# A four-layer perceiver on one core: layer 3's keys and values made ahead in layer 2's self-attention, and scores on 64 feature rows in layers 2 and 3

## The reference

```
# layer 2: x = x + xattn(layernorm(x), ctx, bias)
q, k, v = heads(x_q @ Wq.T), heads(ctx @ Wk.T), heads(ctx @ Wv.T)
p = softmax(q k^T / sqrt(8) + bias[b, h]);  o = p v
...  # then its own norm, a 512-wide gelu part and a second norm
# layer 2 self-attention: softmax(q k^T) + relative position bias, over the 64 tokens of a pair
# layer 3: x = x + xattn(layernorm(x), ctx), with bq, bk, bv, bo and no bias over positions
```

## Time and profile before

| | us |
|---|---|
| median of 3 runs | 1271.48 (1268.71 to 1274.01) |
| profiled execution, first to last instruction (span) | 1270.3 |
| PE busy in it | 1149.3 (90%) |
| DVE, ACT, POOL busy | 697.9, 613.0, 380.3 |

### The profile page before, as it was taken

One profiled execution on the slowest core, in us unless ns is written; L12 is line 12 of the kernel. 1 busy time (PEld: TensorE's weight loads), 2 busy tenths in 40 slices (PEclk: granted clock), 3 DMA queues, 4 the chain that ended last, 5 costly groups with the idle time before them and its releaser, 6 DMA issues.

```text
span 1270.3 us, 27700 instructions
## 1 busy us (share of the span) xinstructions
PE 1149.3 (90%) x9353; PEld 829.9 (65%) x9353; DVE 697.9 (55%) x2032; ACT 613.0 (48%) x1296; POOL 380.3 (30%) x551
## 2 busy tenths in 40 slices
PE   7879999999998879999988268899999999999888
PEld 4446666878785546788865054577777667888655
DVE  5674455554554543777775163533333346777673
ACT  4542224434333433777764132534343446777663
POOL 2300002111121274455540160304040505555350
PEclk9979999999999789999999669999999999999999
DMA  8600121222220003355520301011211110111100
GB/s 251 235 1 25 38 67 32 54 52 52 62 68 1 2 1 108 103 149 145 146 68 1 50 3 42 26 50 50 61 45 56 50 55 22 31 33 29 30 3 17
DMA packets 64837, 73.53 MB, mean 58 GB/s; under 512 B 6144, under 2 KB 57392, under 8 KB 64376
## 3 DMA queue, kind: packets, MB, share of 16 engines
q1 hardware_dynamic: 61480, 64.03, 18.6%
q0 software_dynamic: 1376, 7.49, 1.8%
q10 hardware_dynamic: 1904, 0.98, 0.5%
HBM read 69.86 MB, written 0.52 MB: 55 GB/s over the span
## 4 chain that ended last, share of the span: by engine, by line
PE 77%; DVE 7%; ACT 6%; issue 4%; POOL 3%; DMA 3%; ACTq 1%; POOLq 0%; SPq 0%; DVEq 0%
PE PS L504 14%; PE PS L516 13%; PE PS L1096 8%; PE PS L791 4%; PE PS L755 4%; PE PS L1106 4%; PE PS L507 2%; PE PS L798 2%; PE PS L742 2%; PE PS L1079 2%; ACT AR L1263 2%; PE PS L1126 2%; PE PS L1086 2%; ACT XN L1263 2%; DMA AR<-AR 1%
## 5 line engine op out<-in xcount | busy, mean ns | idle before, releaser
L516 PEld LDWEIGHTS PS<-WB,AR 128*128 128x128 f32 x1568 | 189.9, 192 | 43.6 <-issue 39.5
L516 PE MATMUL PS<-WB,AR 128*128 128x128 f32 x1568 | 190.1, 275 | 0.0
L1263 ACT ACTIVATE AR<-PS,WB 128x512 f32<-128x512 f32 x160 | 110.0, 688 | 153.2 <-PE PS L504 146.7
L1096 PE MATMUL PS<-AR 128*128 128x257 f32 x512 | 138.5, 393 | 2.6 <-POOL AR L2645 2.5
L1855 DVE SCALAR_TENSOR_TENSOR ACC<-PS,SM,ACC 128x128 f32<-128x128 f32 x192 | 54.1, 344 | 95.3 <-PE PS L516 94.3
L1730 DVE TENSOR_TENSOR AR<-PS,AR 128x512 f32<-128x512 f32 (+2 forms) x71 | 49.8, 701 | 96.9 <-ACT AR L1263 40.7
L1096 PEld LDWEIGHTS PS<-AR 128*128 128x128 f32 x512 | 87.1, 190 | 22.5 <-issue 8.0
L504 PE MATMUL PS<-ZT,WB 128*128 128x512 f32 x208 | 101.0, 609 | 0.0
L504 PE MATMUL PS<-XNT,WB 128*128 128x512 f32 x168 | 86.5, 621 | 5.5 <-ACT AR L1263 5.5
L1263 ACT ACTIVATE AR<-PS 128x512 f32<-128x512 f32 (+2 forms) x83 | 43.7, 527 | 89.5 <-PE PS L507 70.9
L2589 POOL TENSOR_TENSOR AR<-AR,SM 128x516 f32<-128x516 f32 x32 | 33.8, 1055 | 155.5 <-ACT SM L1263 93.8
(11 more groups left out here) (320 smaller groups left out, 2184.7 us busy)
## 6 DMA issues: line engine op xcount, KB each, us to landing
WB<-in_units SPq DMA_DIRECT2D x49, 385.0 KB, 3.1
CTX<-in_fside SPq DMA_DIRECT2D x32, 514.0 KB, 3.9
CTX<-in_ctxT SPq DMA_DIRECT2D x96, 130.0 KB, 2.1
CTX<-in_ctxN SPq DMA_DIRECT2D x32, 129.0 KB, 2.3
CTX<-in_ctxN SPq DMA_DIRECT2D x4, 516.0 KB, 7.3
AR<-in_ctxN SPq DMA_DIRECT2D x4, 516.0 KB, 10.6
AR<-in_ctxN SPq DMA_DIRECT2D x32, 64.5 KB, 3.1
AR<-in_l1x_w POOLq DMA_DIRECT2D x1, 2048.0 KB, 8.1
```

Of the source, the lines that this page charges most:

```text
L516: m = pe.matmul(PS[:, 4 + hh, 128 * t:128 * t + 128], f_h[hh][:, c, 128 * t:128 * t + 128], WB[:, q, 2 * UNIT + 128 * c:2 * UNIT + 128 * c ...
L1096: m = pe.matmul(PS[:, 2 + g, 0:KEYS], x_qb[q][:, P * g:P * g + P], x_k[q], start=True, stop=True)
L1263: return act.activation(o, i, fn, **k)
```

## The change

- **Scores on 64 rows (layers 2 and 3).** `x_score` uses the 64 feature rows that hold the group's 32, so groups 0 and 1 use the upper half of the array and groups 2 and 3 the lower. The groups are paired 0 with 2 and 1 with 3, everywhere: order of the scores, banks, maximum, exponentials, transposes.
- **Keys and values of 24 batches kept.** `AR` grows by 6192 columns. Batches 20 to 31 are projected while the pair DMAs run (`kv_early` on PE, taken by DVE), batches 8 to 19 at the end of the self-attention in place of `keep_clock(2, 8)` (`kv_late`, taken by DVE, six of the values by ACT). SP loads the contexts for it into `CTX` after layer 2's cross attention.
- **Layer 3's cross attention** makes keys and values for batches 0 to 7 alone; PE's 32 batches are written out (`x_stored`), ACT and DVE loop over the stored ones.
- Some semaphores are shared under new names.

```diff
-        AR = sb("AR", [P, 18432])
+        AR = sb("AR", [P, 24624])
...
+        x_at = lambda g: 256 * (g % 2) + P * (g // 2)
+        x_bank = lambda g: 2 + 2 * (g % 2) + g // 2
+        kv_T = [CTX[:, :, :].rearrange("p a n -> p (a n)")[:, KPAD * j:KPAD * j + KPAD] for j in range(19)]
+        kv_slot = lambda b: b - 20 if b >= 20 else b + 4 if b < 15 else b - 15
+        kv_k = lambda b: ar(12312 + KV * (b - LIVE), KEYS)
+        kv_v = lambda b: ar(12312 + KV * (b - LIVE) + KEYS, 256).rearrange("p (c n) -> p c n", c=2)
...
# SP
             load_units("l2x")
+            sp.wait_ge(sig["xmax"], seen.up("xmax", 0))
+            sp.wait_ge(sig["xs_ready"], seen.up("xs_ready", 0))
+            kv_load(20, 12, "keys_landed0")
+            kv_load(8, 7, "keys_landed1")
             sp.wait_ge(sig["pair_staged"], 2)
             sp.wait_ge(sig["pair_staged_d"], 1)
             for u in range(1, H, 2):
                 sp.dma_start(*to_pairs(u)).then_inc(sig["pair_landed"], 16)
+            sp.wait_ge(sig["pair_landed"], 16 * H)
+            sp.wait_ge(sig["kv_ready"], 24)
+            kv_load(15, 5, "keys_landed2")
             sp.wait_ge(sig["c_out"], seen.up("c_out", 4))
...
-            sp.wait_ge(sig["xmax"], seen.up("xmax", 0))
-            sp.wait_ge(sig["xs_ready"], seen.up("xs_ready", 0))
-            x_loads(False)
+            sp.wait_ge(sig["kv_ready"], 48)
+            for b in range(LIVE):
+                x_load(b, b % 4, b >= 4, False)
...
# PE
+            def kv_project(b, k):
+                pe.matmul(PS[:, k, 0:KEYS], w("l3x_k"), kv_T[kv_slot(b)][:, 0:KEYS], start=True, stop=True)\
+                    .then_inc(sig["kv_ready"], 1)
+                for c in range(2):
+                    m = pe.matmul(PS[:, k + 1, P * c:P * c + P], kv_T[kv_slot(b)][:, P * c:P * c + P], w("l3x_v"),
+                                  start=True, stop=True)
+                m.then_inc(sig["kv_ready"], 1)
+            def kv_early():
+                pe.wait_ge(sig["w_l3"], 16)
+                pe.wait_ge(sig["keys_landed0"], 32)
+                for n in range(12):
+                    if n == 0:
+                        pe.wait_ge(sig["pair_staged"], 1)
+                    elif n == 1:
+                        pe.wait_ge(sig["pair_staged_d"], 1)
+                    else:
+                        pe.wait_ge(sig["kv_taken"], 2 * n - 2)
+                    kv_project(20 + n, 2 + 2 * (n % 2))
+            def kv_late():
+                pe.wait_ge(sig["keys_landed1"], 32)
+                pe.wait_ge(sig["keys_landed2"], 32)
+                for n in range(12):
+                    if 3 <= n < 9:
+                        pe.wait_ge(sig["kv_taken"], 24 + 2 * (n - 2))
+                    elif n >= 9:
+                        pe.wait_ge(sig["kv_taken"], 36 + n - 8)
+                        pe.wait_ge(sig["kv_taken_a"], n - 8)
+                    kv_project(8 + n, 2 * (n % 3))
...
                 m.then_inc(sig["bias_turned"], 1)
+                kv_early()
                 for half in range(2):
                     pe.wait_ge(sig["pair_v"], half + 1)
                     c_values(6 + half, 2, c_v[:, 512 * half:512 * half + 512])
                 taken("ck_taken", "ck_taken_d", "bias_taken_r")
+                pe.wait_ge(sig["kv_taken"], 24)
...
-                    m = pe.matmul(PS[:, 2 + g, 0:KEYS], x_qb[q][:, P * g:P * g + P], x_k[q], start=True, stop=True)
-                    if g % 2:
+                    r = slice(64 * (g // 2), 64 * (g // 2) + 64)
+                    m = pe.matmul(PS[:, x_bank(g), 0:KEYS], x_qb[q][r, P * g:P * g + P],
+                                  (x_k[q] if keys is None else keys)[r], start=True, stop=True)
+                    if g > 1:
                         m.then_inc(sig["xs_ready"], 1)
...
                         x_score(q, 0, start)
-                        x_score(q, 1, start)
+                        x_score(q, 2, start)
...
-                        x_score(q, 2, start)
+                        x_score(q, 1, start)
                         x_score(q, 3, start)
...
+                def x_stored(b):
+                    q = b % 2
+                    keys = kv_k(b) if b >= LIVE else None
+                    pe.wait_ge(sig["xqb"], seen.up("xqb"))
+                    x_score(q, 0, b == 0, keys)
+                    x_score(q, 2, b == 0, keys)
+                    if b:
+                        x_turn(1 - q, 0)
+                    if b + 1 < LIVE:
+                        x_keys((b + 1) % 4)
+                    if b:
+                        x_turn(1 - q, 1)
+                    x_score(q, 1, b == 0, keys)
+                    x_score(q, 3, b == 0, keys)
+                    if b + 1 < LIVE:
+                        x_values((b + 1) % 4)
+                    if b:
+                        x_pv((b - 1) % 4, b == 1, b == LIVE, kv_v(b - 1) if b > LIVE else None)
...
-            keep_clock(2, 8)
+            kv_late()
             pe.wait_ge(sig["pair_out_landed"], 16 * 11)
...
# ACT, before the norm that follows project(ZT)
+            prepare(ACT.Sqrt)
+            for n in range(6, 12):
+                kv_take(n)
             norm(carried_tile, Z, 0.0)
...
# DVE, after it staged the keys of the pairs
+            def kv_take(b, n, k, values=True):
+                dve.wait_ge(sig["kv_ready"], 2 * n + 1)
+                dve.tensor_scalar(kv_k(b), PS[:, k, 0:KEYS], col("l3x_bk"), None, ALU.add).then_inc(sig["kv_taken"], 1)
+                if values:
+                    dve.wait_ge(sig["kv_ready"], 2 * n + 2)
+                    dve.tensor_copy(kv_v(b), PS[:, k + 1, 0:256].rearrange("p (c n) -> p c n", c=2))\
+                        .then_inc(sig["kv_taken"], 1)
+            for n in range(12):
+                kv_take(20 + n, n, 2 + 2 * (n % 2))
             dve.wait_ge(sig["pair_landed"], 16 * H)
...
             attend(True)
+            for n in range(12):
+                kv_take(8 + n, 12 + n, 2 * (n % 3), n < 6)
             layernorm(carried_tile, Z, True)
```

More of the change, by code:

```diff
@@ L35 @@
 LN_EPS = 1e-5
+LIVE = 8
+KV = 513
 L0X_STEPS = B // 4
@@ L1104, in x_turn, with x_pv @@
                     for c in range(2):
-                        for g in (2 * pair, 2 * pair + 1):
-                            m = pe.transpose(PS[:, 6 + pair, 256 * c + P * (g % 2):256 * c + P * (g % 2) + P],
+                        for g in (pair, pair + 2):
+                            m = pe.transpose(PS[:, 6 + pair, 256 * c + P * (g // 2):256 * c + P * (g // 2) + P],
                                              x_p[q][:, g, P * c:P * c + P], ident)
                     m.then_inc(sig["xpt_ready"], 1)
-                def x_pv(k, first=False, last=False):
+                def x_pv(k, first=False, last=False, values=None):
                     q = k % 2
+                    v = x_v[k] if values is None else values
                     if last:
@@ new lines, in cross @@
+                if biased:
+                    x_four(first=True)
+                    seen.loop(B // 4 - 2, {f"ctx_landed{k}": 32 for k in range(4)} |
+                              {"xmax": 8, "xexp": 16, "xsum_spread": 8, "xt_ready": 12} |
+                              {k: 4 for k in "xk_taken xv_taken xqb xpt_a xpt_d".split()}, lambda i: x_four())
+                    x_four(last=True)
+                    x_turn(1, 0, last=True)
+                    x_turn(1, 1, last=True)
+                    x_pv(3, last=True)
+                else:
+                    pe.wait_ge(sig["kv_taken"], 24 + 18)
+                    pe.wait_ge(sig["kv_taken_a"], 6)
+                    for b in range(B):
+                        x_stored(b)
+                    x_turn(1, 0, last=True)
+                    x_turn(1, 1, last=True)
+                    x_pv(3, values=kv_v(B - 1))
@@ L1635, in cross @@
                 x_four(first=True)
-                seen.loop(B // 4 - 2, {"xexp": 16, "xmax": 8, "xpt_ready": 8} |
-                          {k: 4 for k in "xk_ready xk_taken xpt_a xu_ready".split()}, lambda i: x_four())
-                x_four(last=True)
+                if bk:
+                    for _ in range(LIVE // 4 - 2):
+                        x_four()
+                    x_four(last=True)
+                    seen.loop((B - LIVE) // 4, {"xexp": 16, "xmax": 8, "xpt_ready": 8, "xpt_a": 4, "xu_ready": 4},
+                              lambda i: x_stored())
+                else:
+                    seen.loop(B // 4 - 2, {"xexp": 16, "xmax": 8, "xpt_ready": 8} |
+                              {k: 4 for k in "xk_ready xk_taken xpt_a xu_ready".split()}, lambda i: x_four())
+                    x_four(last=True)
                 x_turned()
@@ L2351, in cross, with x_stored @@
                     per.pop("dve_ran")
-                seen.loop(B // 4 - 2, per, lambda i: x_four(i + 1))
-                x_four(B // 4 - 1, last=True)
+                if biased:
+                    seen.loop(B // 4 - 2, per, lambda i: x_four(i + 1))
```

(14 more changed lines are left out.)

76 lines of the change are left out of this document (41 added, 35 removed).

## The result

The changed kernel takes 1252.76 us (median of 4 runs, 1246.0 to 1256.47) against 1271.49 before; the ratio is 0.986, interval 0.9818 to 0.9902. Forecast were 1257 and a range of 1239 to 1272.

What follows compares the result with a forecast made beforehand. PE alone was taken to make layer 3's period, with DVE as good as full in layer 2. -2.5-1.0-13.2+1.4+1.0 = -14.3 on a 1270.3 us span gave 1256.0, with 1.2 more 1257; range 1239 to 1272.

Steps and rivals of the forecast that it cites:

- Score tiles: Layers 2 and 3: 64-row score pairs overlap, 0.435 instead of 0.87 each; PE's step with keys 4.12, 0.25 less.
- Rival (B): Score pairs overlap only in part, 0.22 more a pair; keyed step 4.56, total 1270; chance 0.14.
- Rival (C): Two 64-row score tiles do not overlap at all; keyed step 5.0, total 1286; chance 0.09.
- Layer 2: Layer 2's cross attention: DVE holds the step at 4.36 against 4.44, gaining 2.5 us (0 to 6.5).
- Eight batches with keys: Layer 3's batches still making keys and values: PE leads, 4.2 against 4.37 in six steps, gaining 1.0 us.
- Stored batches: Layer 3's 24 batches with kept keys and values: 3.82 a step against 4.37, gaining 13.2 us (10 to 17.5).
- the loop through POOL: Stored batches: waits through DVE's tail, POOL's six operations and PE take 7.50 for two steps, 3.75 each.
- The 3.64 that I called the next loop: Layer 3's final batch before: a loop through DVE's copy, maximum, ACT's exponentials and PE's transposes gives 3.64 a step.
- Early and late: Moved projections: 12 early batches cost nothing during the pair DMAs; 12 late ones cost 1.4 us (0.5 to 3).
- Program code: PE's written-out 32 batches: "issue" stalls in straight code cost 1.0 us.
- Rival (D): PE's written-out code stalls, costing up to 16 us; total 1262 to 1272; chance 0.06.
- Rival (A): Both cross attentions: PE is all that counts and other engines' loops slacken; total 1231; chance 0.15.

Runs made afterwards that it cites:

- e3: The kernel before with scores on 64 rows but in the old pairs, both matmuls on the same half of the array; 1300.55 us.
- e5: The changed kernel with DVE's two loops over the batches written out as straight code; layer 2 took 125.4 us against 134.6.
- e2: The changed kernel with scores on all 128 rows again, new pair order kept; layer 2 137.4 us, inner stored steps 3.92 on average.
- e4: The changed kernel with POOL spreading the queries ahead of the tail of the batch before; 1256.6 us, inner stored steps 3.76 instead of 3.85.
- e7: The changed kernel with the batch loops of DVE, POOL, ACT and PE written out and POOL's queries ahead of the tail; ratio 0.978 to the kernel before.
- e8: The changed kernel with the 12 early projections and their DVE takes done twice; ratio 0.9921 to the kernel before.
- e6: The changed kernel with the batch loops of DVE, POOL, ACT and PE written out; layer 2 124.9 us, stored steps 3.65 on average.
- e10: The kernel before, its cross-attention batch loops written out on four engines and POOL's queries ahead of the tail, nothing of the change; 1269.99 us.

## Why the prediction was right

The forecast case came true, and the sum for layers 2 and 3 with it: they gave 17.4 where 16.7 was summed. Within that sum layer 2 and the split of layer 3 came out by errors that cancel.

**Score tiles.** Taken at 0.435 and 0.2 a pair, and measured so (0.64). A keyed PE step is 4.05 where 4.12 was counted. Rival (B), partial overlap, falls with the 0.64. Rival (C)'s price was right as well: its condition, no overlap, gave 4.91 in e3 where it said 5.0. That each tile spans all columns made no difference to the overlap. "TensorE: Matmul & The Clock Gate" of the Trainium skill, Part 3 (matmuls start in program order), would have made a pair 0.65 without the switch; 0.64 with it disagrees, if a matmul's two records are taken as two matmuls in a row.

**Layer 2.** 2.9 gained, 2.5 forecast, and DVE named. But the reason was half wrong: I took 4.27 for the work of DVE. e5 shows that this work fits in 4.05 with 0.4 to spare, and that 4.36 is the form of the code: waits inside a hardware loop and its turn. I had the turn (0.46) and not the waits. The bound of 6.5 that I gave, "if PE with the turns set it", was too small for what was there: 12.1 in e5. Nor did the gain lie where the sum put it, evenly at 0.08 a step. Within the loops (steps 5 to 27) a step fell from 4.51 to 4.46, 1.1 us in all; the first four and the last four steps, in straight code, gave 1.8, with steps of 4.05 among them where I had taken 4.27. That the two errors met at 2.9 is luck; what held is that DVE and not PE binds the middle.

**Eight batches with keys.** 1.0 forecast; five steps at 4.05 give 5 x 0.32 = 1.6, and the sixth, in which the first stored batch already comes in, took 3.47 and gave 0.9 more. These steps run on straight code on DVE and ACT, which is why coupling cost nothing.

**Stored batches.** Forecast 3.82 a step by the loop through POOL, measured 3.85 inside; with a pair of 0.87 on that loop the same sum said 3.94, measured 3.92 (e2). The 3.64 that I called the next loop was not the next floor: e4 shows DVE's turn there, and e7 reaches 3.49, so that 3.64, read at the last batch, holds idle time that is no part of the loop; which was not looked into. The gain was 11.9, not the 13.2 of the sum: of its 24 steps the last was already without keys and values before (3.74 in the earlier trace rows), so 23 gained 0.52 each. The 1.5 more in the keyed steps made up for it.

**Early and late.** Nothing and 1.4 forecast; nothing moved at the pairs (69.84 us from layer 2's last sums to PE's next work there, 70.06 before), and the late work cost 0.3 to 1.5. What e8 leaves open is whether more early work costs something behind the pairs.

**Program code.** 1.0 forecast; in the changed kernel's written-out steps I found none, and with all engines' code written out (e7) the inner steps still repeat to 0.01 us. e5, e6 and e10 have single steps that are 0.1 to 0.4 longer than their neighbours, of unknown cause. Rival (D), a stall every other step, did not come.

**Rival (A)**, that PE is all that counts, said 1231, 41.5 less in the two layers. It needed the loops to slacken; they did not. With them written out and the queries first, e7 has 35.7 less. What failed in (A) was PE alone at 3.1 for the stored steps; the copy by DVE keeps them at 3.49.

**The total.** 1252.76 against 1257: 0.7 from the layers and 1.0 from the code that did not stall explain 1.7. The other 2.5 is within what the clock does from run to run; of the profiles' difference of 22.3 the clock made 9.3 ahead of layer 2, and took back 4.4 between the layers.

## What to carry to other kernels

When one engine stops being the bound, look at the code form of the next one: here DVE was held not by its operations but by its hardware loops, and the stored steps by the order of POOL's work as well. Writing the loops out and spreading the queries first raised what the change was worth in the two layers from 17.4 to 33.3 us. The price of a step with work taken out can be estimated beforehand by adding up the loops through the other engines (3.82 against 3.85 here); a last step that already lacks the work is no floor by itself (3.64 read, 3.49 reached). Where a sum comes out right, look whether each of its terms did. Where the clock varies between runs, compare stretches between fixed marks at full clock; whole times hid gains of 2 and of 6 us here (e4, and e7 over e5). Where whole times and stretches disagree (e8), neither alone settles it.

## What the runs showed of the hardware

- In a hardware loop, DVE idles 0.15 behind its own writes, 0.22 ahead of a step and 0.67 at the turn; in straight code the next operation starts about 0.04 after the last one's end. Over layer 2 that is 9.2 us (134.6 to 125.4). Waits there are on values that a register computes; which part is the wait and which the loop was not measured apart.
- Two score matmuls of 64 rows on different halves of the array start 7 ns apart and take the time of one (0.435 and 0.2 for the switch); on the same half they take 0.87 and the switch. Half the rows alone save nothing.
- A switch of tile shape cost 0.14 to 0.20 in each of the five places of e3's step.
- Unchanged code took 32 us at a granted clock of 0.69 in one run and 24 at 1.00 in another; runs of one kernel spread 16 us with it.
